# Last states kept by ScalarE, separate product rings, and a layer norm whose sums ScalarE accumulates, in a Mamba layer

## The reference

```python
def step(h, inp):
    dt_t, B_t, C_t, u_t = inp
    dA = jnp.exp(dt_t[:, :, None] * A)
    h = dA * h + (dt_t * u_t)[:, :, None] * B_t[:, None, :]
    y = jnp.einsum('bdn,bn->bd', h, C_t)
    return (h, y)
...
y = ys.transpose(1, 0, 2) + u * Dskip
y = y * jax.nn.silu(z)
return jnp.einsum('bti,oi->bto', y, out_w)
...
for l in range(N_LAYERS):
    residual = x
    h = _mamba_layer(x, in_proj_w[l], conv_w[l], ...)
    h = _layer_norm(h, ln_w[l], ln_b[l])
    x = h + residual
```

## Time and profile before

| | us |
|---|---|
| median of three runs | 9800.02 |
| lowest, highest | 9798.58, 9802.13 |
| the profiled execution, its own time | 9793.81 |
| its span, first to last instruction | 9791.9 |
| Mamba layer 0, from its first scan | 4829 to 6930 |
| Mamba layer 1, from its first scan | 6960 to 9072 |

### The profile page before, as it was taken

The page is one execution under the profiler, slowest core; times in us unless marked ns, Lnnn a source line. Parts: engine busy times, 40 slices in busy tenths (PEclk is TensorE's granted clock), DMA queues, the critical chain, the costliest instruction groups (busy, mean ns, idle before and its releaser), DMA issues. The chain is left out here.

```text
span 9791.9 us, 174268 instructions
## 1 busy us (share of the span) xinstructions
PE 8306.5 (85%) x48396; PEld 4746.0 (48%) x48396; DVE 8402.3 (86%) x13204; ACT 5594.2 (57%) x9153; POOL 4993.0 (51%) x4685
## 2 busy tenths in 40 slices
PE   4559999999999998499688888888688888888599
PEld 1236666767666766366333333333233333333366
DVE  3558888888888887699599999999599999999799
ACT  1237777777777775133366666666466565565233
POOL 0000000000000000188499999999599999999487
PEclk7779999999999999799899999999899999998799
DMA  5568888888888888311122211112122222211111
GB/s 179 199 223 279 281 282 280 280 282 282 280 283 281 280 281 254 101 43 42 66 77 79 79 71 63 68 77 79 54 84 88 88 88 88 81 73 73 44 43 40
DMA packets 1172883, 1448.23 MB, mean 148 GB/s; under 512 B 81370, under 2 KB 1052650, under 8 KB 1139728
## 3 DMA queue, kind: packets, MB, share of 16 engines
q1 hardware_dynamic: 1172560, 1445.22, 44.8%
HBM read 881.86 MB, written 564.60 MB: 148 GB/s over the span
## 5 line engine op out<-in xcount | busy, mean ns | idle before, releaser
L1914 POOL TENSOR_TENSOR mb_bx<-mb_dtu,mb_bc 128x512 f32<-128x512 f32 x2048 | 2662.0, 1324 | 9.8 <-DVE mb_hs L2014 9.7
L2157 PE MATMUL mb_y_ps<-mb_g,ident 128*128 128x512 f32 x4096 | 2196.5, 643 | 461.2 <-DVE mb_g L1974 237.7
L2201 ACT ACTIVATE mb_dA<-mb_dt,mb_a_neg 128x512 f32<-128x512 f32 x2048 | 1400.7, 688 | 1628.0 <-DVE mb_hs L2014 1089.8
L1350 POOL MEMSET f_magic<- 128x1 f32 x2 | 0.2, 98 | 3625.7 <-POOLq L127 3625.7
L2157 PEld LDWEIGHTS mb_y_ps<-mb_g,ident 128*128 128x128 f32 x4096 | 765.2, 199 | 1646.7 <-issue 726.3
L961 ACT ACTIVATE at_tab<-at_e_ps 128x384 f32<-128x384 f32 x2064 | 1011.9, 490 | 806.9 <-PE at_e_ps L878 805.8
L1015 DVE TENSOR_REDUCE at_nmax<-at_s_ps 128x1 f32<-128x1024 f32 x1025 | 1255.0, 1224 | 35.1
L894 PE MATMUL at_pT_ps<-ident,at_probs 128*128 128x128 f32 x8192 | 1115.7, 279 | 100.3 <-ACT at_probs L966 81.4
L966 ACT ACTIVATE at_probs<-at_s_ps,at_nmax 128x1024 f32<-128x1024 f32 x1025 | 1140.9, 1113 | 61.1 <-DVE at_nmax L1015 39.3
L894 PEld LDWEIGHTS at_pT_ps<-ident,at_probs 128*128 128x128 f32 x8192 | 894.7, 141 | 402.2 <-ACT at_probs L966 373.4
L1974 DVE TENSOR_TENSOR mb_g<-mb_hs,mb_bc 128x512 f32<-128x512 f32 x1472 | 992.8, 674 | 40.1 <-PE mb_y_ps L2157 38.7
(11 more groups left out here) (236 smaller groups left out, 14171.1 us busy)
## 6 DMA issues: line engine op xcount, KB each, us to landing
at_tables<-at_tab SPq DMA_DIRECT2D x1032, 384.0 KB, 4.0
at_skew<-at_tables SPq DMA_DIRECT2D x1030, 256.0 KB, 3.1
mb_bc<-mb_bc_rows SPq DMA_DIRECT2D x256, 1024.0 KB, 6.3
at_skew<-at_tables SPq DMA_DIRECT2D x773, 128.0 KB, 3.5
at_opnd<-at_q_st SPq DMA_DIRECT2D x130, 210.0 KB, 4.6
at_opnd<-at_kl_st SPq DMA_DIRECT2D x130, 210.0 KB, 4.8
at_opnd<-at_kr_st SPq DMA_DIRECT2D x130, 210.0 KB, 4.7
at_q_st<-st_parts SPq DMA_DIRECT2D x96, 256.0 KB
```

The lines of the kernel that those rows point to most:

```text
L1914: pool.tensor_tensor(bx[:, s % RINGS, :], dtu[:, c, :], bc[:, 0, n, :], ALU.mult).then_inc(s_bx, 1)
L2157: nc.tensor.matmul(y_ps[:, c % 2, :], ident[:, :], g[:, s1 % RINGS, :], start=False, stop=(n == STATE - 1)).then_inc(s_y, 1)
L2201: nc.scalar.activation(dA[:, s % DA_RING, :], dt[:, c, :], ACT.Exp, scale=a_neg[:, c, n:n + 1]).then_inc(s_dA, 1)
```

## The change

Three things are done, all in `mamba_layer`.

1. **Last states.** The copy into `carry` goes from DVE to ACT (`keep_carry`, before `dA` of step s, for step s-2), in even items. DVE's product of a step waits for ACT's copy of that step's state in even items.
2. **Rings.** `g` of four becomes `g_dve` of three (`G_DVE`) and `g_pool` of two (`G_POOL`). PE adds POOL's products five steps after their step (`SUM_LAG_POOL`) and no longer in order of steps. Who waits for sums counts them in the new order (`sums_to`). POOL's product p waits for the sum of POOL's product p-2, DVE's product d for that of d-3. `combine` of chunk 3 goes from step 4 to 7. The softplus writes its parts straight into `dt` and `dtu` (the buffers `v`, `e`, `lnp` go), and SP's wait for sums stands only before the C half of a group.
3. **Output norm.** The reads of the output projection also give row sums (`accum_out`), POOL makes minus the mean of them at 25 (L1998), ACT squares the centred rows at 28 and 29 with accumulated sums, and POOL makes variance, `pow` and shift at 30 (four operations, each waiting for the one before). `bn_stats` and `bn_aggr` of this norm go; the input norm of layer 0 keeps its own. The centring goes from 33, 34 to 34, 35.

```diff
-AT_Y = (29, 38, 54, 4)
-AT_ONORM, AT_OCENTER, AT_OSCALE = 26, (33, 34), 44
+AT_Y = (29, 38, 54, 7)
+AT_OMEAN, AT_OSQUARE, AT_OVAR, AT_OCENTER, AT_OSCALE = 25, (28, 29), 30, (34, 35), 44
+G_DVE, G_POOL = 3, 2
+SUM_LAG_POOL = 5
+def sum_order(s):
+    return (s + (SUM_LAG_POOL if s in TIMES_C_POOL else 1), s in TIMES_C_POOL)
+def turned_over(i, ring, count):
+    return i - ring if i >= ring else max(range(i % ring, count, ring)) - count
...
+        def summed(t, s):
+            return t.n * SLOTS + sums_to(s, t.n_static == 0, t.n_static == items - 1)
+        def product_read(eng, t, slots, i, ring):
+            i = turned_over(i, ring, len(slots))
+            if i >= 0 or t.n_static != 0:
+                t = t if i >= 0 else t.plus(-1)
+                ge(eng, s_y, summed(t, slots[i]))
...
                             sp.wait_ge(s_bx, k.n * SLOTS + (IC - 1) * STATE + n + 4)
-                            sp.wait_ge(s_y, k.n * SLOTS + (IC - 1) * STATE + n + 4)
                         for i in range(2):
+                            if i == 1 and not first_body(k):
+                                at = (IC - 1) * STATE + n
+                                sp.wait_ge(s_y, summed(k, max(range(at, at + 4), key=sum_order)))
...
-                            ge(pool, s_y, m1 - RINGS + 1)
-                            pool.tensor_tensor(g[:, s1 % RINGS, :], state(s1), bc[:, 1, s1 % STATE, :],
+                            product_read(pool, t, by_pool, p, G_POOL)
+                            pool.tensor_tensor(g_pool[:, p % G_POOL, :], state(s1), bc[:, 1, s1 % STATE, :],
...
+                    if tail and s == AT_OMEAN:
+                        pool.wait_ge(s_oc, t.n * QT + QT)
+                        pool.tensor_tensor(omean[:, :], osum[:, :], over[:, 0, :], ALU.mult).then_inc(s_omean, 1)
...
-                if t.u == 0:
-                    nc.vector.tensor_copy(carry[:, s1:s1 + 1], state(s1)[:, BANK - 1:BANK])
                 if s1 not in TIMES_C_POOL:
-                    ge(dve, s_y, m - RINGS + 1)
+                    if t.u == 0:
+                        dve.wait_ge(s_carry, t.j * SLOTS + s1 + 1)
+                    product_read(dve, t, by_dve, d, G_DVE)
...
-                        if s == AT_ONORM:
-                            dve.wait_ge(s_oc, b.n * QT + QT)
-                            norm_stats(o_sb, 1).then_inc(s_ochain, 1)
-                        if s == AT_ONORM + 1:
-                            dve.wait_ge(s_ochain, done + 1)
-                            norm_aggr(1).then_inc(s_ochain, 1)
...
+                    if s >= SUM_LAG_POOL and scan or s < SUM_LAG_POOL and tail:
+                        lag = s - SUM_LAG_POOL
+                        t, s1 = (k, lag) if lag >= 0 else (b, SLOTS + lag)
                         if s1 in TIMES_C_POOL:
+                            pe.wait_ge(s_gp, t.n * TC_POOL + p + 1)
+                            nc.tensor.matmul(y_ps[:, c % 2, :], ident[:, :], g_pool[:, p % G_POOL, :],
+                                             start=False, stop=(s1 == last_summed(c))).then_inc(s_y, 1)
...
+                def keep_carry(k, s):
+                    t, s1 = (k, s - DA_RING) if s >= DA_RING else (b, SLOTS + s - DA_RING)
+                    if t.u == 0:
+                        nc.scalar.activation(carry[:, s1:s1 + 1], state(s1)[:, BANK - 1:BANK], ACT.Copy).then_inc(s_carry, 1)
...
                         nc.scalar.activation(o_sb[:, i, :], ring[:, ring_bank("out", i, k, -1), 0:D],
-                                             ACT.Copy).then_inc(s_oc, 1)
+                                             ACT.Copy, accum_out=osum[:, i:i + 1]).then_inc(s_oc, 1)
...
+                            ins = nc.scalar.activation(sq[:, i, :], o_sb[:, i, :], ACT.Square, bias=omean[:, i:i + 1],
+                                                       accum_out=osq[:, i:i + 1])
```

105 lines of the change are left out of this document (71 added, 34 removed).

## The result

The changed kernel takes 9903.68 us (median of four, 9888.17 to 9908.82) against 9799.3 of before on the same chip: ratio 1.0106, interval 1.0094 to 1.0119, or +104 us. The forecast was slower, +37, with a range up to 9885. The sign was right, the size was not, and the time lies above the range. (The prediction's own sum is 36; the 37 is a slip of rounding.)

The account below looks back on a forecast made before the run. The prediction took POOL as the bound, or level with DVE, around the output norm's statistics; 12 + 27 - 16 + 8 + 5 = +36 us gave a forecast median of 9837 us, own range 9810 to 9865, widened to 9738 to 9885.

Parts of the forecast that it names:

- the C half's cover: POOL's bx 12 may wait one or two us for the load; POOL's 1.82 us slack at step 24 covers it: 0.
- Part 1: Output norm's statistics leave DVE, 51 us of work in all; gain nothing, because POOL bounds that stretch.
- part 2: POOL's added small operations for the output norm: 0.38 us an item, +12 us.
- the 17.5 forecast: Sign of being right: the scan of step 35 comes no earlier than 17.5 us after that of step 26.
- the waits for `bx` in steps 27 to 31: Sign of being right: DVE waits there for POOL's bx, by 1 to 1.6 us.
- Rival (a): DVE is the bound after all, so work taken from it shows: 9698 to 9780 us; chance 0.23.
- Part 3: Ring of two and late sums: POOL's product at step 24 waits for one more PE sum, +27 us.
- the mechanism at step 24: Seven PE sums instead of six precede POOL's product 21, making it 0.86 us later an item.
- The wait at 24: Sign of being right: POOL's wait for PE at step 24 grows to about 2.7 us.
- Part 4: Last states from DVE to ACT in even items: -16 us on DVE, +8 on ACT.
- Part 5: Combine moved to step 7 stands behind DVE's wait in odd items, 0.3 us each: +5 us.
- Rival (c): PE at half clock before the dt projection in even items too: +26, 9863 us or more; chance 0.20.

Follow-up runs that it names:

- e3: The kernel before with only the output norm's sums and squares moved to ACT; ratio 1.0015, +15 us.
- e1: The kernel before with only the rings and late sums (last states stay on DVE, norm keeps bn_stats); ratio 1.0070, +69 us.
- e7: e1 with POOL's ring of three products instead of two; ratio 1.0033, +32 us against the kernel before.
- e8: e1 with separate semaphores for the B and C halves of a load; ratio 1.0051, +50 us against the kernel before.
- e13: e1 with the edits of e7 and e8 and combine of chunk 1 at step 42, sums still five steps late; ratio 0.9951, -48 us against before.
- e14: The kernel before with rings, sums in order, last states split between ACT and DVE, steps 61 to 63 on DVE; ratio 0.9955, -44 us.
- e2: The kernel before with only the last states copied by ACT instead of DVE; ratio 1.0022, +22 us.
- e10: e1 with sums in order and combine of chunk 3 back at step 4; ratio 0.9956, -43 us against the kernel before.
- e17: The changed kernel with DVE keeping the last states of steps 61 to 63; ratio 1.0087, +85 us against the kernel before.
- the four pairs above: Pairs differing in whether ACT or DVE copies steps 61 to 63; time over ten turns 63.5 against 42.2, 69.3/45.7, 53.8/42.5, 60.2/51.7 us.

## Why the prediction missed

What failed are terms that the prediction put at nothing or left out: the wait of `combine` of chunk 1 for a late sum (+29 us around step 38 in the trace), the loop's turn behind the copies on ACT (+18), the C half's cover, and PE's clock at the output projection (some 20).

**Part 1 (statistics off DVE: 0)** and **part 2 (norm on POOL: +12)**: right. 0.41 us an item in e3's trace for a forecast 0.38, and +15 in time. The scan of step 35 came 17.74 us after that of 26 (5979.00 - 5961.26), no earlier than the 17.5 forecast, and the waits for `bx` in steps 27 to 31 are 0.64 + 0.64 + 0.22. Rival (a), DVE as the bound, is out. It had drawn on DVE being as busy as POOL in layer 1; from first to last scan DVE has 1937.0 us and POOL 1970.3 of 2055.2, so that they are busy 94 and 96% and POOL is ahead there too.

**Part 3 (ring and late sums: +27)**: the mechanism at step 24 was right and its size too: 13.71 - 12.86 = 0.85 us for 0.86, the same in every item at the full clock, and from scan 23 to scan 38 e1 takes 25 us more than before, where 27 were forecast. Three steps around it failed.

- I looked at whose buffer waits for which sum, and not at who else waits for all of them. `combine` of chunk 1 stands at step 38 and needs the sum of step 31, which now stands at PE's step 36. In the changed kernel PE ends it at 5988.20 and DVE has waited 2.73 us. The prediction spoke only of the `combine` that was moved, chunk 3's, and not of those that stayed where they were; 0.6 to 1.1 us an item of that wait were still there at step 42, by the four groups of items (even and odd, layer 0 and 1).
- The C half and `bx` 12 at 0: the wait of one or two us came as said (48.9 us in all), but its cover, POOL's slack at step 24, was not spare: in e7, where the wait for sums is gone, the wait for the load grows by 26 us, and only with e8's edit and `combine` at 42 on top does the kernel come to e13's -48. How much it costs by itself isn't shown; e8's 19 us are within the noise.
- The wait at 24 was to grow to 2.7 us, and it is 1.55, since POOL comes later. The marker was badly chosen: a wait on a late engine shrinks. The distance from PE's release to POOL's product is the marker that holds.

I also took the rings and the lateness as one thing. e1 with its sums in order is -52 and the lateness +121, and nothing in the change ties them together.

**Part 4 (last states: -16 + 8)**: measured +22, so the sum has the wrong sign. DVE's -16 is a gain that no run shows (e14), since where DVE leads, the next wait is for PE or `dA`. (The Trainium skill, page Perfetto Trace Analysis, section Optimizing Scalar/DVE Operations, with its 125 ns for a DVE operation on PSUM would have made it 40, an estimate; the copies of the kernel before stand 0.05 us ahead of the product behind them, and no run shows a gain of either size.) Two more terms were missing. Of the DVE wait that the change adds I named what is queued behind it, the next scan, for all steps alike; at step 62 what is queued behind it is DVE's jump, and what it waits for stands behind ACT's: some 10 to 20 us with the new rings. And the copies make ACT's read of the convolution later, so that PE waits 2.07 us and not 1.82 and more items run at the lower clock: 8 us in e2's trace by the estimate above. What makes up the rest of e2's 22 is open.

**Part 5 (`combine` at 7: +5)**: not confirmed; e10 says 0 or a small gain.

**Rival (c)**, PE at the lower clock in even items, was right in kind and wrong in place: not before the `dt` projection but at the output projection, where PE's idle time rose from 1.82 to 2.07 us and the projection from 1.99 to 3.33. It gave DVE's wait of 1.35 at step 17 and 0.9 us at step 24 in even items of layer 0, and it is there in all seven of them in which PE waits, but only in one of the seven of layer 1, where PE idled 1.87 to 2.44 us. e2 has the same 2.07 in even items, at the lower clock in one of six in layer 0 and in four of six in layer 1. So why the clock falls in some and not in others is open.

Open is also the item's end in layer 0: the changed kernel loses 1.3 us there in even items, with DVE's first scan waiting 3.45 by "issue" (above), and e17 does so as well without any copy behind the jump. In e17 the gain lies in layer 1: 15.6 us of it, and 2.8 in layer 0, from first to last scan. That fits the copy: in the changed kernel DVE's product of step 62 waits for it, 0.2 to 0.6 us, at four of the five turns of layer 1 and at none of layer 0. In layer 1 the time over the turns falls from 37.7 to 17.0 us.

## What to carry to other kernels

When an operation is done later, list everyone who waits for it or for a count that includes it, also those that the change doesn't touch: here `combine` of another chunk, which no line of the change touches, holds 26 of the 110 us that the late sums cost in the traces, and a load's second half took up what a longer ring gave back. Where several waits come from one lateness, each alone gives little when removed, because the others stand right behind; price them together, and test them together. And a wait must not cross a loop's jump: what an engine does last in a pass should not need what another does first in the next.

## What the runs showed of the hardware

- A turn of the loop costs time even when nothing new waits there. From the last scan ahead of it to the first behind it, it is 2.4 to 8.5 us in all kernels here, and 1.7 to 2.0 at the same place in unrolled passes. The kernel before spends 45.8 us on its ten turns; at 1.8 each they would be an estimated 18. In the four pairs above, the kernel in which DVE's product ahead of the turn needs ACT's copy behind it has 9 to 24 us more there; e2 has 3 more than the kernel before.
- An accumulated output on ACT is a second instruction in the trace, 128x1 and 193 ns in the mean (24.7 us for 128 of them), behind an activation that takes as long as without it (367 ns against 365). Where the next activation follows without a wait it starts 0.09 us after it. No run prices it alone.
- A copy of 128x1 by ACT is 167 ns long from PSUM and 200 from SBUF, and the `dA` behind it starts 0.05 to 0.07 us later from PSUM and 0.09 to 0.11 from SBUF, where nothing is waited for.
- After waits of 1.7 to 2.4 us PE's output projection ran at a granted clock of 0.56 to 0.74 in 14 of 28 items of the changed kernel, and at full clock in the others. At the lower clock it took 2.4 to 3.5 us and not 1.99, and the item was 1.3 to 1.9 us longer from scan 13 to scan 26.
